# Embedding weights and first images as one input tensor, loaded in four half-partition chunks; new instruction sequences on four engines

## What is computed

```python
h = patches @ W.T + b                                    # 1024 x 768 -> 256
v = h @ w1.T + b1
w = softmax((v @ ww.T + bw).reshape(T, B, 16, 31))       # 16 heads, 31 taps
y = causal_conv(v, w)                                    # along the image axis
a = layer_norm(h + y @ w2.T + b2, gamma, beta)
h = layernorm(h + a)
gate = silu(bitlinear(h, w_gate)); up = bitlinear(h, w_up)   # 256 -> 1024
h = layernorm(h + bitlinear(gate * up, w_down))              # 1024 -> 256
```

## Time and profile before

| | us |
|---|---|
| median of 3 runs (120.03 to 121.67) | 121.08 |
| the profiled execution | 120.99 |
| its span in the trace | 119.2 |
| PE busy | 104.6 (88%) |
| DVE, ACT, POOL busy | 79.2, 69.2, 79.3 |

### The profile page before, as it was taken

How to read it: one execution, slowest core, us unless ns; L and a number is a source line. 1 busy time by engine, 2 the same in 40 slices (tenths; PEclk the granted TensorE clock), 3 DMA queues, 4 the chain that set the end, 5 groups by cost and what they waited for, 6 DMA issues and landing times.

```text
span 119.2 us, 2371 instructions
## 1 busy us (share of the span) xinstructions
PE 104.6 (88%) x716; PEld 66.7 (56%) x716; DVE 79.2 (66%) x187; ACT 69.2 (58%) x124; POOL 79.3 (67%) x147
## 2 busy tenths in 40 slices
PE   6949999999999999999999999999999988775300
PEld 2538367768756475676746756666665754443200
DVE  5301974445646575577978997887978899788510
ACT  0042019826293036359536997887688799788520
POOL 6995000020259799998997488788888889888830
PEclk9999999999999999999999999999999999999955
DMA  3999999962223231220132130224310000010231
GB/s 98 348 308 354 432 392 425 403 256 35 24 58 37 55 31 43 25 28 1 50 28 32 39 32 6 58 27 99 35 32 29 0 0 0 3 43 19 69 89 53
DMA packets 22532, 12.20 MB, mean 102 GB/s; under 512 B 18036, under 2 KB 20596, under 8 KB 22135
## 3 DMA queue, kind: packets, MB, share of 16 engines
q1 hardware_dynamic: 21436, 10.39, 31.0%
q10 hardware_dynamic: 1082, 1.65, 4.2%
HBM read 9.70 MB, written 2.34 MB: 101 GB/s over the span
## 4 chain that ended last, share of the span: by engine, by line
PE 61%; POOL 16%; DMA 8%; issue 6%; DVE 3%; ACTq 1%; POOLq 1%; DVEq 0%
PE bank L356 13%; PE bank L431 11%; PE bank L414 11%; PE bank L397 6%; PE bank L458 5%; DMA bias_row<-in_bias 4%; POOL q L1118 4%; DMA xT<-in_xT 3%; PE bank L489 3%; PE bank L505 3%; POOL f L1125 3%; POOL rstd L1032 2%; PE bank L544 2%; PE bank L412 2%; PE bank L444 1%
## 5 line engine op out<-in xcount | busy, mean ns | idle before, releaser
L1083 POOL TENSOR_TENSOR taps<-probs,inv_total 128x256 f32<-128x256 f32 x8 | 5.1, 636 | 22.2 <-DVE inv_total L792 22.1
L356 PE MATMUL bank<-xT,tokW 128*128 128x256 f32 x72 | 16.6, 380 | 0.0
L431 PE MATMUL bank<-conv_w,vpad 128*32 128x128 f32 x256 | 15.8, 399 | 0.0
L356 PEld LDWEIGHTS bank<-xT,tokW 128*128 128x128 f32 x72 | 13.6, 190 | 3.5 <-issue 1.8
L414 PE MATMUL bank<-wl,h1T 128*128 128x496 f32 x32 | 14.6, 578 | 0.0
L431 PEld LDWEIGHTS bank<-conv_w,vpad 128*32 128x32 f32 x256 | 8.2, 122 | 6.1 <-issue 2.5
L666 ACT ACTIVATE gu<-bank,sc 128x512 f32<-128x512 f32 x16 | 11.0, 685 | 1.2 <-PE bank L489 1.1
L854 DVE TENSOR_TENSOR gu<-gu,bank 128x512 f32<-128x512 f32 x16 | 10.9, 681 | 1.0 <-ACT gu L666 0.8
L1118 POOL TENSOR_SCALAR q<-gu,sc 128x512 f16<-128x512 f32 x14 | 9.9, 708 | 1.3
L771 DVE TENSOR_REDUCE top<-bank 128x16 f32<-128x496 f32 x8 | 5.4, 672 | 8.0 <-PE bank L414 8.0
L544 PE MATMUL bank<-w_q,q2T 128*128 128x256 f16 x64 | 8.4, 272 | 2.4 <-ACT q2T L680 2.0
(11 more groups left out here) (120 smaller groups left out, 231.5 us busy)
## 6 DMA issues: line engine op xcount, KB each, us to landing
xT<-in_xT SPq DMA_DIRECT2D x3, 768.0 KB, 13.7
w_raw<-in_wg SPq DMA_DIRECT2D x1, 1024.0 KB, 10.7
w_raw<-in_wu SPq DMA_DIRECT2D x1, 1024.0 KB, 12.7
w_raw<-in_wd SPq DMA_DIRECT2D x1, 1024.0 KB, 15.6
shear<-taps SPq DMA_DIRECT2D x8, 128.0 KB, 1.7
conv_w<-shear SPq DMA_DIRECT2D x64, 16.0 KB, 1.9
out_dram<-res SPq DMA_DIRECT2D x7, 128.0 KB
ww<-in_ww SPq DMA_DIRECT2D x1, 496.0 KB, 5.7
```

The lines of the kernel that those rows point to most:

```text
L356: last = nc.tensor.matmul(ps_embed(pair, m), tokW[:, k, m * P:(m + 1) * P], xT[:, pair, k, :], start=(k == 0), stop=(k == KC_PATCH - 1))
L431: last = nc.tensor.matmul(ps_yT[j * SLOT:(j + 1) * SLOT, k, :], vpad[:, s, h, :], conv_w[:, s, :, h], start=(par == 0), stop=(par == 1))
```

## The change

**Loads.** `tokW` and the first pair's images become one input tensor `first` of 128 x 6 x 512 numbers, so that a contraction block of a partition is one row of 2 KB where it was one of 1 KB in each of two tensors. It is loaded in four chunks of 1, 1, 2 and 2 blocks; SP's queue issues partitions 0 to 63 of each chunk, ACT's queue partitions 64 to 127. SP no longer waits for a chunk before it issues `ww`, and ACT no longer waits before its next DMAs. On ACT's queue the three bias rows come before `w1o`.

```diff
-FIRST = [0, 1, 3]
+FIRST = [0, 1, 2, 4]
...
             for i, (k0, k1) in enumerate(zip(FIRST, FIRST[1:] + [KC_PATCH])):
-                sp.dma_start(tokW[:, k0:k1, :], tokW_d[:, k0:k1, :]).then_inc(tokW_in[i], 16)
-            sp.wait_ge(tokW_in[1], 16)
+                sp.dma_start(first[0:P // 2, k0:k1, :], first_d[0:P // 2, k0:k1, :]).then_inc(first_in[i], 16)
             sp.dma_start(ww[:], ww_d).then_inc(ww_in, 16)
...
                     if k in FIRST:
-                        pe.wait_ge(tokW_in[FIRST.index(k)], 16)
-                        pe.wait_ge(x0_in[FIRST.index(k)], 16)
+                        pe.wait_ge(first_in[FIRST.index(k)], 32)
...
             for i, (k0, k1) in enumerate(zip(FIRST, FIRST[1:] + [KC_PATCH])):
-                act.dma_start(xT[:, 0, k0:k1], xT_d[0, :, k0:k1]).then_inc(x0_in[i], 16)
+                act.dma_start(first[P // 2:P, k0:k1, :], first_d[P // 2:P, k0:k1, :]).then_inc(first_in[i], 16)
             act.dma_start(bias_cols[:], cols_d).then_inc(cols_in, 16)
-            act.wait_ge(x0_in[1], 16)
-            act.dma_start(w1o[:], w1o_d).then_inc(w1o_in, 16)
             act.wait_ge(bias_zero_ok, 1)
             for j in range(3):
                 act.dma_start(bias_row[32 * j:32 * j + 1, :], bias_d).then_inc(bias_in, 16)
+            act.dma_start(w1o[:], w1o_d).then_inc(w1o_in, 16)
```

More of the change, by code:

```diff
@@ L226, in vit_tower @@
         last_ok = sem("last_ok")
+        last_scale_ok = sem("last_scale_ok")
         q2_last_ok = sem("q2_last_ok")
@@ L559, in _ @@
                 nc.tensor.matmul(bank[7][:, :], ones_bf[:], ones_bf[:, 0:1].broadcast_to([P, 512]), start=True, stop=True)
-            first_embeds(); logit_weights(); logit_bias(); residual(0); values(0); embed(1, 0); logits(0)
-            embed(1, 1); logits(1); embed(2, 0); weight_means(0, 2); logits(2); embed(2, 1); logits(3); conv(0)
-            values(1); project_out(0); logits(4); conv(1); residual(1); values(2); weight_means(2, 3)
-            project_out(1); logits(5); residual(2); conv(2); embed(3, 0); in_transposes(0); project_out(2)
@@ L569, in _ @@
-            down(1, 0); down(1, 1); project_out(5); gate(3, 0); up(3, 0); values(6); in_transposes(4); up(3, 1)
-            gate(3, 1); residual(6); conv(6); values(7); project_out(6); gate(4, 0); up(4, 0)
-            inner_transposes(2, 0); inner_transposes(2, 1); up(4, 1); gate(4, 1); residual(7); conv(7)
+            first_embeds(); logit_weights(); logit_bias(); values(0); residual(0); embed(1, 0); logits(0)
+            embed(1, 1); logits(1); weight_means(0, 2); embed(2, 0); weight_means(2, 3); logits(2); embed(2, 1)
@@ new lines, in _ @@
+            logits(3); conv(0); values(1); project_out(0); logits(4); residual(1); conv(1); values(2)
+            project_out(1); embed(3, 0); residual(2); logits(5); conv(2); values(3); in_transposes(0)
+            project_out(2); gate(0, 0); up(0, 0); embed(3, 1); up(0, 1); gate(0, 1); residual(3); conv(3)
+            logits(6); in_transposes(1); project_out(3); gate(1, 0); up(1, 0); inner_transposes(0, 0)
+            in_transposes(2); inner_transposes(0, 1); up(1, 1); gate(1, 1); values(4); down(0, 0); residual(4)
@@ new lines, in _ @@
+            inv_std_mid(4); add_beta(5); out_scales(4); scale_h3(3); inv_std_attn(5); quant_inner(2, 0)
+            quant_inner(2, 1); shift_result(0); inv_std_mid(5); add_beta(6); add_h3(1); quant_inner(3, 0)
+            out_scales(5); scale_h3(4); inv_std_attn(6); inv_std_out(1); quant_inner(3, 1); shift_result(1)
+            inner_limit(4); inner_limit(5); inv_std_mid(6); add_beta(7); add_h3(2); out_scales(6)
+            inv_std_attn(7); quant_inner(4, 0); quant_inner(4, 1); inner_limit(6); scale_h3(5); inv_std_mid(7)
```

148 lines of the change are left out of this document (73 added, 75 removed).

## The result

The changed kernel is slower: 123.70 us median of 4 runs (122.44 to 124.67) beside 121.38 for the kernel before on the same chip, a ratio of 1.019 with a 95% interval of 1.013 to 1.025. That it is slower is clear of noise; whether it reaches the two per cent at which the prediction calls a kernel slower is not. The forecast was 119.5, and its range ended at 121.0. The profiled execution of after took 123.67 us, with a span of 121.9 (before: 119.2). Of every kernel, executions more than 1.5% above its fastest are left out of the ratios, and since those profiled for e4 and e11 are among them, nothing is read from these two profiles.

A forecast was written before the change was run, and what follows sets the result against it. The prediction took PE to bound the kernel, full from 15.2 to 93.9 us, leaving only the two ends: 120.99 - 1.55 (earlier `logit_bias`) + 0.1 (the end) = 119.5 us, range 117.9 to 121.0.

The forecast's parts named there:

- Where it is decided: PE, full from 15.2 to 93.9 us, can only move as a block; gains lie at the two ends.
- `conv(0)`, `weight_means(2, 3)` and `gate(0, 0)`: Middle of the kernel: three checks for new PE waits once the block moves 1.55 us earlier; each taken at cost 0.
- The end: From `inv_std_attn(7)` on, POOL's list changes in one point and gets 0.1 us longer.
- the moved scale: POOL's list at the end: `scale_h3(5)`, 0.48 us, comes behind `inv_std_attn(7)`, and `out_scales(6)`, 0.39, moves ahead.
- The gain of the chunks: Loads at the start: longer rows gain 0.4 us (0 to 0.7), so the last chunk lands at 8.3.
- brings nothing: Rival at the start: halves leave the rate at 359 GB/s, `ww` bounds, gain only 0.8; 120.4 us, chance 0.13.
- The first chunk is there at 3.6 in both kernels: Start: all 24 passes in a row from about 3.6 us give 9.0 as the embedding's earliest end.
- 0.225 us per pass: End of the embedding: 8 passes behind the last chunk take 1.8 us, so it ends at 10.1.
- earlier issue, for `ww`: Start: `ww` issued at about 2.5 us instead of 5.16, gaining 0.9 and landing at 10.0.
- The bias rows: Start: no longer behind `w1o`, they come 1.5 us earlier (1.1 to 1.8), so DVE starts at 10.0.
- 13.6 for `b_ww`: Start: DVE's 3.6 us make `b_ww` ready at 13.6, together with PE; `logit_bias` starts then instead of 15.14.
- The slower one: Rival: ACT's third sum waits for the last megabyte, holding PE at `weight_means(2, 3)`; slower by 2%, 123.5 us, chance 0.05.

The follow-up runs named there:

- e4: The changed kernel with `w1o` ahead of the bias rows on ACT's queue; four runs took 122.18 to 125.13 us.
- e11: The kernel before with the bias rows ahead of `w1o` on ACT's queue, the wait for the second chunk kept; ratio 1.005.
- e1: The kernel before (old loads) with the new sequences and `last_scale_ok` alone; 121.72 us, ratio 1.005.
- e3: The changed kernel with each chunk as one DMA of 128 partitions, chunks 0 and 2 on SP's queue, 1 and 3 on ACT's; 121.59 us, ratio 1.001.
- e6: e3 with nine warm-up matmuls instead of six; 121.23 us, ratio 1.004.
- e17: e16's loads with the new sequences of the change; 120.36 us, ratio 0.998.
- e2: The new loads of the change with the old sequences; 123.63 us, ratio 1.016.
- e10: The kernel before with four warm-up matmuls instead of six; 120.93 us, ratio 0.999.
- e13: e6 with the old sequences; 121.05 us, ratio 0.998.
- e16: The changed kernel with old sequences, first chunk split by columns, the others whole, `w1o` on SP ahead of `ww`; 120.19 us, ratio 0.995.
- e19: e16 with the two DVE instructions that make `b_ww` moved ahead of those for the bias rows; 119.46 us, ratio 0.990.
- e14: The changed kernel with `w1o` issued by SP ahead of `ww`; 122.30 us, ratio 1.012.
- e15: The changed kernel with SP's and ACT's waits for the second chunk put back; 121.57 us, ratio 1.002.
- e18: e16 with the bias rows ahead of the last chunk on ACT's queue; 120.58 us, ratio 1.000.

## Why the prediction was wrong, point by point

- **Where it is decided: right.** PE is full from `logit_bias` to the last tile in both kernels, and the middle moved as a block, by 2.6 us, though the other way. `conv(0)`, `weight_means(2, 3)` and `gate(0, 0)` opened no wait.
- **The end: right in sign, small in size.** +0.2 us for +0.1. From `inv_std_attn(7)` to the end it is 24.3 to 24.5 us in after, e1, e3, e6 and e17, which have the new sequences, and 24.1 to 24.4 in before, e2, e10, e13, e16 and e19, which have the old; that the moved scale is the reason was not tested.
- **The gain of the chunks: the step that failed first.** It read 359 and 430 GB/s off as rates of shorter and longer rows and placed the halves between them. The 359 is one microsecond; from 3 to 9 us the kernel before moved 326. The halves ran at 274. The last chunk came at 10.4 and not at 8.3. The rule on halves that it cites from the Trainium skill ("DMA: Bandwidth & Descriptors", Rules for kernel authors) says that they run on the same engines as one whole transfer, and the prediction took it for "brings nothing" (120.4). Whole chunks (403 GB/s in e3) show that here they lose; of a loss the prediction had no term. "The first chunk is there at 3.6 in both kernels" failed with it: SP's half was there at 3.62, ACT's at 4.21. And 0.225 us per pass was read from a profile whose clock had risen at 4.02; no term stood for a later rise, which in after adds about 0.25 us, because passes were still outstanding when the last chunk came (8 passes from 10.4 would have ended at 12.2, not 12.45), and in e3, where the last chunk came at 7.6, is what keeps the embedding until 12.5.
- **w1o: the step that is missing.** The prediction noted that the bias rows no longer stand behind its 256 KB and never asked where `w1o` itself would then land, although `logit_weights` needs it. It landed at 14.2 instead of 9.2. By working, with the end of the embedding counted as in the prediction to where the next step can begin: it came 2.35 us late (12.45 for 10.1), `w1o` added 1.9 (14.35), and `logit_weights` took 0.1 less than counted, together 4.15, the whole of 17.75 - 13.6. e14 takes away the 1.9 alone, and e15, by two waits, most of the loss in the median. The forecast also started from a profile in which `w1o` came early: with the same loads it landed at 13.3 in e1. That SP's and ACT's waits hold other bytes back from what is urgent was not in the change's list of costs at all: it counted their removal as earlier issue, for `ww`, which was issued at 3.26 (forecast about 2.5) and landed at 11.2 and not at 10.0.
- **The bias rows: wrong twice.** They did not come earlier, and had they come at 10.0, DVE's 3.6 us would have begun to count at about 10.6, behind POOL's memset. The forecast's 13.6 for `b_ww` was not to be had with DVE's order as it was (e6, e13, e17, e18: 14.15). The row of that memset was in the trace of before, hidden there because the bias rows came at 11.48.
- **The rivals.** The slower one was put on ACT's third weight sum, which played no part. No slower one was put on the start, where all the loads were reordered.

That the last part of the mechanism is sound, an earlier logit_bias moves the whole block, shows in e19: with whole chunks behind the first, `w1o` in time, `b_ww` first and the old sequences, logit_bias starts 1.8 us earlier than before, at 13.36, and the ratio is 0.990. That its median, 119.46, is the 119.5 of the forecast is chance: the kernel before ran at 120.50 beside it, and the change itself gives nothing of this.

## What to carry to other kernels

When a change reorders loads, list for every consumer step all the tensors it needs, and give each its new landing, also those that only moved backwards; a wait ahead of an issue may be what keeps later bytes off an urgent load. Share a transfer between two queues in whole pieces of 128 partitions, not in partition halves. When a wait is about to vanish, look at what the waiting engine would meet if it started earlier, another engine's long instruction too. And a profile is one execution: what a forecast takes from it as a fixed landing (`w1o` at 9.2) or a fixed rate (0.225 us per pass) may differ in the next.
